# The last two laps of attention and the router behind them, written out in an order of their own on each engine

## The reference

```python
x = adapter(x, cond)                          # low rank, modulated by cond
h = layernorm(x)
q, k, v = split(h @ w_qkv + b_qkv)            # 16 heads of 8
attn = softmax(q @ k.T / sqrt(8))             # within a sequence of 128 tokens
x = x + (attn @ v) @ w_o + b_o
h = layernorm(x)                              # "post" in the kernel
logits = h @ gate_w + gate_b                  # 8 experts
topv, topi = top_k(logits, 2); gw = softmax(topv)
moe = sum over the 2 chosen experts of gw * (relu(h @ W1[e] + b1[e]) @ W2[e] + b2[e])
return x + moe
```

## Time and profile before

| | us |
|---|---|
| three runs | 777.63, 775.84, 770.14 |
| median | 775.84 |
| profiled execution, its own time | 771.82 |
| its span in the trace | 769.0 |
| TensorE busy | 617.8 (80%) |
| VectorE busy | 474.6 (62%) |
| GpSimd busy | 431.3 (56%) |
| ScalarE busy | 383.4 (50%) |

### The profile page before, as it was taken

One profiled execution on the slowest core, in us unless ns is written; L12 is line 12 of the kernel. 1 busy time (PEld: TensorE's weight loads), 2 busy tenths in 40 slices (PEclk: granted clock), 3 DMA queues, 4 the chain that ended last, 5 costly groups with the idle time before them and its releaser, 6 DMA issues.

```text
span 769.0 us, 17719 instructions
## 1 busy us (share of the span) xinstructions
PE 617.8 (80%) x5541; PEld 490.0 (64%) x5541; DVE 474.6 (62%) x1520; ACT 383.4 (50%) x838; POOL 431.3 (56%) x573
## 2 busy tenths in 40 slices
PE   5797885977778648875999999999972499999882
PEld 2455554977778636552666666666651399999882
DVE  3535344654554556755787787678645477886576
ACT  4323321443444417775767777677632256664441
POOL 2565652455555566634444777877756245664443
PEclk9899988999999957996999999999995599999997
DMA  7999814664656551854493435343101698888747
GB/s 241 221 278 320 236 38 128 187 178 132 169 156 176 169 205 63 249 182 136 126 263 95 130 83 137 93 132 98 43 29 36 209 284 241 249 252 248 209 154 246
DMA packets 106297, 131.21 MB, mean 171 GB/s; under 512 B 16272, under 2 KB 83888, under 8 KB 106096
## 3 DMA queue, kind: packets, MB, share of 16 engines
q1 hardware_dynamic: 92864, 109.40, 50.3%
q0 software_dynamic: 9088, 18.76, 7.0%
q10 hardware_dynamic: 4272, 2.14, 1.0%
HBM read 80.75 MB, written 49.50 MB: 169 GB/s over the span
## 4 chain that ended last, share of the span: by engine, by line
PE 29%; issue 9%; DVE 6%; POOL 5%; another core or an unknown queue 2%; DMA 1%; SPq 1%; ACT 1%; DVEq 0%; POOLq 0%
PE psO L2040 7%; PE psA L939 6%; PE ps L1872 3%; PE psAO L1902 2%; POOL late_rows L358 2%; PE ps L1882 2%; PE ps L1884 2%; PE psAO L1911 2%; PE psT L889 1%; DMA kp<-qk_parts 1%; POOL rstd L1475 1%; DVE mneg L1727 1%; DVE fh L2064 1%; DVE fo L2051 1%
## 5 line engine op out<-in xcount | busy, mean ns | idle before, releaser
L948 POOL DMA_INDIRECT expert_rows<-fo,to x78 | 80.0, 1025 | 78.3 <-DVE fo L2051 53.6
L948 POOL DMA_INDIRECT expert_rows<-eo,to x78 | 77.0, 987 | 76.8 <-ACT eo L1094 59.5
L1727 DVE TENSOR_REDUCE mneg<-ps 128x4 f32<-128x512 f32 x128 | 86.2, 676 | 48.3 <-PE ps L1872 39.7
L1823 ACT ACTIVATE arena<-ps 128x512 f32<-128x512 f32 x128 | 75.3, 589 | 56.3 <-PE ps L1884 55.6
L358 POOL DMA_INDIRECT dispatch_rows<-row,index x64 | 62.8, 982 | 54.4 <-DVE index L339 37.4
L939 PE MATMUL psA<-xh,wh 128*128 128x256 f32 (+1 forms) x234 | 73.7, 315 | 15.6 <-DVE xl L925 15.0
L921 DVE CAST xh<-psT 128x256 fp32r<-128x256 f32 x78 | 32.7, 420 | 79.6 <-PE psT L889 38.9
L358 POOL DMA_INDIRECT late_rows<-row,index x64 | 64.0, 1000 | 20.3 <-issue 15.1
L1872 PE MATMUL ps<-km,qp 96*128 96x512 f32 x128 | 63.5, 502 | 10.9 <-ACT km L1816 7.3
L1816 ACT ACTIVATE km<-kp,const 96x512 fp32r<-96x512 f32 x96 | 67.8, 713 | 8.3 <-PEq L1180 4.6
L939 PE MATMUL psA<-xh,wl 128*128 128x256 f32 (+1 forms) x234 | 67.1, 287 | 0.0
(11 more groups left out here) (227 smaller groups left out, 1591.0 us busy)
## 6 DMA issues: line engine op xcount, KB each, us to landing
late_rows<-tail SPq DMA_DIRECT2D x17, 1040.0 KB
wb<-in_W1b SPq DMA_DIRECT2D x29, 578.0 KB
w<-in_W SPq DMA_DIRECT2D x29, 304.0 KB
qk_parts<-qk SPq DMA_DIRECT2D x8, 1024.0 KB, 4.6
qp<-qk_parts SPq DMA_DIRECT2D x48, 128.0 KB
kp<-qk_parts SPq DMA_DIRECT2D x48, 128.0 KB
qm<-qk_parts SPq DMA_DIRECT2D x192, 32.0 KB
arena<-in_W1b SPq DMA_DIRECT2D x10, 578.0 KB
```

The costliest lines, as they stand in the source:

```text
L948: pool.indirect_dma_start(out=m.ybuf, out_offset=bass.IndirectOffsetOnAxis(ap=to[b][:, a:a + 1], axis=0), in_=out[b][:, a, :], in_offset=N ...
L1727: nc.vector.tensor_reduce(mneg[s % 2][:, g, :], ps1[:, g % 2, :].rearrange("p (j k) -> p j k", j=4), AX_X, ALU.max, negate=True).then_inc( ...
L1823: nc.scalar.activation(prob[s % 2][:, g, :], ps2[:, g % 2, :], ACT.Exp, scale=ATT_SCALE).then_inc(exped, 1)
```

## The change

The loops over laps stop two laps earlier (`LAPS = SEQS - 2`). What laps 30 to 45 issued is written out behind each engine's loop, in an order of its own. The set of operations is the same, and so is their arithmetic; three helpers are new. `last_mix(g)` takes the place of `mix` and `total` for sequence 31: for one strip g the four matmuls with ones and then the four with values. `choose_late` and `index_late` (VectorE) and `rows_late` (ScalarE) run a group's choice, index and weights in one piece. The gate logits of groups 6 and 7 go to the two banks of `ps1` (`late_banks`) and their ranks to `psM` (`late_rank`). Both joins of groups 6 and 7 stand behind the last scatter.

```diff
-        LAPS = SEQS + 14
+        LAPS = SEQS - 2
+        late_banks, late_rank = [ps1[:, a, 0:2 * (P + E)] for a in range(2)], psM[:, 0:(GT + 1) * E]
+        P5, P6, P7 = GROUPS - 3, GROUPS - 2, GROUPS - 1
+        S0, S1 = SEQS - 2, SEQS - 1
 ...
+                half = range(0, GT * TOPK // 2), range(GT * TOPK // 2, GT * TOPK)
+                part_max(S1)
+                spread_v(S0)
+                post_root(post, pool, P6)
+                post_scatter(post, pool, P5, P5 % 2, half[0])
+                spread_v(S1)
+                post_scatter(post, pool, P5, P5 % 2, half[1])
+                post_scatter(post, pool, P6, P6 % 2, range(0, TOPK))
+                post_root(post, pool, P7)
+                post_scatter(post, pool, P6, P6 % 2, range(TOPK, GT * TOPK))
+                post_scatter(post, pool, P7, P7 % 2)
+                post_join(post, pool, P6)
+                post_join(post, pool, P7)
 ...
+                post_moments(post, dve, P6, kept)
+                invert(S0 - 2)
+                post_gather(post, dve, P6)
+                divide(S0 - 2)
+                post_variance(post, dve, P6)
+                index_late(P5, post.rank_out)
+                spread_max(S1)
+                post_centre(post, dve, P6)
+                keep(S0 - 2)
+                invert(S1 - 2)
+                divide(S1 - 2)
+                keep(S1 - 2)
+                invert(S0)
+                divide(S0)
+                choose_late(P6)
+                keep(S0)
+                invert(S1)
+                divide(S1)
+                index_late(P6, late_rank)
+                keep(S1)
+                post_moments(post, dve, P7, kept)
+                post_gather(post, dve, P7)
+                post_variance(post, dve, P7)
+                post_centre(post, dve, P7)
+                choose_late(P7)
+                index_late(P7, late_rank)
 ...
+                for g in range(HG):
+                    exponent(S0, g)
+                post_normalise(post, act, P6, (0, 1))
+                exponent(S1, 0)
+                post_normalise(post, act, P6, (2, 3))
+                exponent(S1, 1)
+                post_scale(post, act, P6)
+                exponent(S1, 2)
+                exponent(S1, 3)
+                rows_late(P6)
+                post_normalise(post, act, P7, range(GT))
+                post_scale(post, act, P7)
+                rows_late(P7)
 ...
+                def last_mix(g):
+
+                    s, p, out = S1, S1 % 2, slice(32 * g, 32 * g + 32)
+                    pe.wait_ge(exped, HG * s + g + 1)
+                    for j in range(4):
+                        nc.tensor.matmul(psO[out, p, P:2 * P], m.const[:, C_ONESB + 32 * j:C_ONESB + 32 * j + 32],
+                                         prob[p][:, g, j * P:(j + 1) * P], start=(j == 0), stop=(j == 3),
+                                         skip_group_check=True)
+                    for j in range(4):
+                        ins = nc.tensor.matmul(psO[out, p, 0:P], vb[p][:, 4 * g + j, :], prob[p][:, g, j * P:(j + 1) * P],
+                                               start=(j == 0), stop=(j == 3), skip_group_check=True)
+                    if g == HG - 1:
+                        ins.then_inc(mixed, 1)
+
+                shift(S0, 0)
+                mix(S0 - 1, range(4))
 ...
+                project(S0 - 2)
+                shift(S0, 3)
+                total(S0 - 1, range(4))
+                shift(S1, 0)
+                mix(S0, range(4))
+                shift(S1, 1)
+                pe.wait_ge(mxT_done, SEQS)
+                post_turn(post, pe, P6)
+                total(S0, range(4))
+                shift(S1, 2)
+                project(S1 - 2)
+                shift(S1, 3)
+                pe.wait_ge(maxed, HG * SEQS)
+                post_natural(post, pe, P6, late_banks)
+                pe.wait_ge(vb_done, S1 + 1)
+                pe.wait_ge(divided, S1 - 1)
+                last_mix(0)
+                last_mix(1)
+                project(S0)
+                last_mix(2)
+                last_mix(3)
+                post_rank(post, pe, P6, P6 % 2, late_rank)
+                project(S1)
+                pe.wait_ge(post.router.slotted, P6 + 1)
+                post_turn(post, pe, P7)
 ...
+                post_natural(post, pe, P7, late_banks)
+                post_rank(post, pe, P7, P7 % 2, late_rank)
```

23 lines of the change are left out of this document (added).

## The result

The changed kernel takes 780.55 us (median of 7 runs, 779.74 to 785.97), beside 774.64 us for the kernel before (770.14 to 777.63). The ratio is 1.0108, with a 95% interval of 1.0078 to 1.0139, so it is some 8.4 us slower, 6.0 to 10.8; the two medians alone lie 5.9 us apart. The forecast was +2.5 us at 778.3, with a range of 773.0 to 784.0. The time lies inside the range, the sign is right, and the size by the ratio is over three times what the sum gave.

What follows compares the result with a forecast made beforehand. Bound by two chains of small steps, GpSimd's 16 scatters and group 7's own, not by work. Terms +0.5 (`keep`), +2.2 (one stop), -1.1 (`diff`), +0.9 (root) give +2.5 on 775.84: 778.3 us, range 773.0 to 784.0.

Steps and rivals of the forecast that it cites:

- (a): TensorE up to group 6's gate matmul: moved ahead, it ends at 568.3, some 6.5 us earlier than before.
- (b): Sequence 31's mix and total, strip by strip: four `last_mix` take 7.0 us against 2.2 before.
- (c): Group 6's gate matmul to the end of sequence 31's `keep`: choice hidden by `last_mix`; `keep` ends at 578.5, +0.5 us.
- (d): TensorE stopping where group 5's scatters stand close together: one stop, +2.2 us; between none and two, 4.4.
- (e): Joins behind all scatters: VectorE's `diff` in group 7's choice no longer waits, -1.1 us; the joins' own time is hidden.
- (f): Group 7's root on GpSimd, behind two scatters of group 6: starts 2.5 us behind `keep` instead of 1.5, +0.9.
- (g): Lap 30: one project ahead of a shift, group 5's index ahead of `spread_max(31)`; nothing, or 0.3 us at most.
- K after 582: Sign of a wrong forecast: K, the end of sequence 31's `keep` on VectorE, forecast at 578.5, coming later than 582.
- full clock for group 7: Low end of the range: group 7's transposes and gate matmul at full clock, -1.4 us, with no stop; 774.5 us.
- Half clock in the slow mixes: Rival: TensorE's clock falls inside the four `last_mix`, up to 14.0 us, +7.0 more, 785.3 us; chance 0.14.
- Overlap of neighbouring strips: Rival: neighbouring sets of `last_mix` overlap, shrinking its time towards 2.2 us, -4.8, total 773.5; chance 0.10.
- GpSimd's 16 scatters would bind: Rival, nothing moves: scatters of groups 6 and 7 bind; excluded, ending at 602.2 ahead of group 7's 604.9; no chance given.

Runs made afterwards that it cites:

- a3_p5_behind_mix: The changed kernel with group 5's eight scatters held until the last mix ends, group 7's root behind two of them; ratio 1.0114 to the kernel before.
- d1_before_joins_last: The kernel before with only both joins moved behind all scatters, on a chip where the kernel before takes 706 us; ratio 0.9988.
- c1_run_of_six: The changed kernel with group 5's scatters two, spread, six instead of four, spread, four, where the kernel before takes 706 us; ratio 1.0058.

## Why the prediction was right, and where its sum was off

(a) *The gate matmul at 568.3, 9.4 behind A.* Without scatters beside it, it ends 8.65 behind A (`a3_p5_behind_mix`, 571.36), with GpSimd's order as before 9.8. In the changed kernel it ended at 580.22, 18.0 behind A. The working was right; the stop came on top.

(b) *`last_mix` 7.0.* It took 6.9 with the project in it (580.14 to 587.04), at full clock for nearly all of it. The adapter's down product was the right row to price it by, and the Trainium skill's rule on distinct column groups ("TensorE: Matmul & The Clock Gate", "Why this matters for your kernels") pointed the right way: 6.9 us here against 2.2 and a project. Undoing it alone brought 4.5 of K, which is the difference of the two prices.

(c) *10.2 from the gate matmul to K.* 9.2, the same in the changed kernel and in the run without scatters. Group 6's mask was written by 582.23, well ahead of the end of `last_mix`, so the choice was hidden as said.

(d) *Stops, 2.2, at most 4.4.* **This is the step that failed.** Between the changed kernel and the same without scatters beside TensorE lie 27.2 - 17.9 = 9.3 us. The prediction had seen the stop in the rows, had seen that scatters stand close together there, and had noted that the change puts them in fours. It then priced them by a count, one or two of the size of the one in the rows, and the change made the hold itself longer. What sets where a hold ends isn't settled. In the kernel before, finished work came out 1.0 us behind the last of four scatters, as the join ran, and with GpSimd's order as before 0.9 behind it. In the changed kernel one hold ended at 567.3, inside the first four, and the next only 1.2 behind the last of all eight, across the spread between them. Priced from the first scatter to the last the stop would have been 10.4 us (563.69 to 574.13), near the 9.3. But that rule is fitted after the result, and in `a3_p5_behind_mix` a hold ended in the middle of 22 scatters.

(e) *The joins, -1.1.* `diff` is back at 0.17 (600.41), and both joins at the end (from 613.02) hold nothing up, as TensorE's first rows come at 617.27. (f) *The root, +0.9.* It started at 591.73, 2.3 behind K, against the forecast of 2.5. Together K to the expert stage is 0.5 shorter, forecast 0.2. (g) Nothing was seen.

The sum in the terms measured: without holds K would have come 17.9 - 19.1 = -1.3 against before, with its own holds, where the forecast had +0.5; then +9.3 in place of +2.2; then -0.5 in place of -0.2. That gives +7.6 in the profiles against +2.5. The -1.3 is counted against a kernel before that had holds of its own. Without holds its orders take 14.3 from A to K (`d1_before_joins_last`). So of the 8.1 us between A and K some 3.5 (17.9 - 14.3, read across two chips) are TensorE's new order, with the slow mix in it, and the rest, some 4.6, are holds that grew from 4.8 to 9.3. The prediction had the earlier gate matmul pay for nearly all of the slow mix; but that matmul was late in the kernel before by a hold. It ended 16.1 behind A there, and 11.3 in `d1_before_joins_last`.

One of the prediction's own signs of being wrong came: K after 582. It was 589.40, or 586.1 less the 3.3 us that were lost ahead of A. The gate matmul ended at 580.22, not near 568 to 570. Its range also does not follow from its terms: no stop and full clock for group 7 give 774.7, two stops 780.5, where it wrote 774.5 and 781.5. For the -1.4 of full clock it shows no row. And the page gives TensorE's share in slices 29 to 33 as 9, 7, 2, 4 and 9 tenths, not as told ahead of the prediction; no term rests on it.

*The rivals.* Half clock in the slow mixes did not come: the clock fell inside the stop and was at 1.00 from 581. What it cost was the gate matmul at 2.02 in place of 1.09. The forecast's danger was named in the wrong place: the clock was low over 571 to 581 (0.73 and 0.59), in the stop and just behind it, and at full over 581 to 586, with TensorE busy in the slow mix all the while. Overlap of neighbouring strips did not come either, 6.9 against 2.2. That GpSimd's 16 scatters would bind was rightly excluded.

The time lay in the range because this was wide enough, not because the stop was understood. Slower by over 1% had 0.15, and the ratio of 1.0108 is just past that bound.

## What to carry to other kernels

When the trace shows an engine stopped by another's transfers, don't price the stops of a new order by counting those of the old one: list where such transfers will stand beside dense work, and take as the far end a stop from the first to the last of them. Where transfers stand, or a piece of other work such as a join between them, can be worth more than the microsecond it costs on a path (8.2 us of K came back with GpSimd's old order), so don't sweep such work to the end without a look at what stood beside it. Matmuls with small outputs belong in turns over the four strips of 32 partitions; grouping them strip by strip to start earlier cost nothing only where a wait hid the difference. And ask for the time of the kernel before on every chip: the one kernel took 772 and 706 us on two of them, and the change costs 8.4 us on the one and by its nearest relative (`c1_run_of_six`) about 4 on the other.

## What the runs showed of the hardware

Where the kernel before takes 772 to 775 us (the first measurement, of which the record has no chip number, and one chip in two sets of runs), GpSimd's indirect scatters (0.96 us each, 0.30 apart) hold what TensorE has finished. In most rows the hold ends 0.5 to 1.2 us behind the last of a run of them, in some inside the run. The longest is 6.7 us in the changed kernel's profile. TensorE's issue falls into bursts after 52 to 59 records. Not every completion beside a scatter is held: group 7's transposes came out within 0.05 us. On the two chips where it takes 706 us the same scatters at the same pace hold nothing in attention, and a change that costs 8.4 us on the one kind, over half of it by holds, should by `c1_run_of_six` cost about 4 on the other. What sets the two kinds of chip apart, and how much of the 42 us ahead of attention is such holds, the runs don't show. Matmuls of 128x32 weights on 128 fp32 columns took 0.11 us a record when all wrote one strip of 32 partitions, and 0.025 when they took turns over four.
